# The last batch's tail in a new order on every engine: cross attention with a mixture of experts behind it

## The reference

```python
out = retention(LN(x), ctx, ctx)      # 16 heads of 16, decaying causal scores, chunked in the kernel
x = x + out
x = x + fp8_gemm(LN(x), kernel)       # rounded to e4m3, then a plain product
q, k, v = x_n @ Wq.T, ctx @ Wkv.T     # 16 heads of 16
attn = softmax(q @ k.T * 16 ** -0.5)
x = x + (attn @ v) @ Wproj.T + bproj
logits = LN(x) @ router.T             # 8 experts, the best 4 of each token, softmax over these
gate, up = split(x_n @ gate_up[e].T + b)
act = (clip(up) + 1) * min(gate, 7) * sigmoid(1.702 * gate)
out = x + sum over chosen e of w[e] * (act @ down[e].T + b)
```

## Time and profile before

| | |
|---|---|
| median of three runs | 963.2 us (957.24, 965.97, 963.2) |
| profiled execution, its own time | 960.33 us |
| its span, first to last instruction | 958.5 us |
| mean granted TensorE clock | 0.892 |
| TensorE busy | 785.8 us (82%) |
| VectorE, ScalarE, GpSimd busy | 635.5 (66%), 480.4 (50%), 281.9 us (29%) |

### The profile page before, as it was taken

One profiled execution on the slowest core, in us unless ns is written; L12 is line 12 of the kernel. 1 busy time (PEld: TensorE's weight loads), 2 busy tenths in 40 slices (PEclk: granted clock), 3 DMA queues, 4 the chain that ended last, 5 costly groups with the idle time before them and its releaser, 6 DMA issues. The chain is left out here.

```text
span 958.5 us, 19166 instructions
## 1 busy us (share of the span) xinstructions
PE 785.8 (82%) x6449; PEld 489.9 (51%) x6449; DVE 635.5 (66%) x1288; ACT 480.4 (50%) x977; POOL 281.9 (29%) x260
## 2 busy tenths in 40 slices
PE   0682677779887888998978789779999999999994
PEld 0441333233332533342323225567898889888883
DVE  5545656787658787788688975357667766556552
ACT  1210310445334363435675752545777777777772
POOL 6005100310030100001000004125678566566543
PEclk9996779668989799797998986889999999999997
DMA  8321263013221144010454511032354344343332
GB/s 285 115 72 44 99 198 101 34 43 115 71 68 66 40 121 129 2 51 23 134 167 167 165 39 46 23 134 52 64 134 74 63 69 66 55 70 66 58 42 34
DMA packets 70779, 81.41 MB, mean 85 GB/s; under 512 B 10080, under 2 KB 64224, under 8 KB 70560
## 3 DMA queue, kind: packets, MB, share of 16 engines
q1 hardware_dynamic: 56864, 61.01, 20.1%
q0 software_dynamic: 13824, 19.18, 12.3%
HBM read 51.65 MB, written 28.51 MB: 84 GB/s over the span
## 5 line engine op out<-in xcount | busy, mean ns | idle before, releaser
L381 PE MATMUL gu_ps<-xt_room,w 128*128 128x256 f16 (+1 forms) x2112 | 214.8, 256 | 5.9 <-ACT xt_room L276 5.4
L1170 DVE TENSOR_REDUCE neg_max<-sc 128x2 f32<-128x1024 f32 x128 | 156.4, 1222 | 60.7 <-PE sc L1509 59.8
L381 PEld LDWEIGHTS gu_ps<-xt_room,w 128*128 (+1 forms) x2112 | 178.4, 99 | 31.6 <-issue 8.2
L1802 POOL DMA_INDIRECT out<-y,block_rows x72 | 119.7, 1663 | 78.9 <-ACT y L1771 41.6
L2099 PE MATMUL misc<-w,h_room 128*128 (+1 forms) x864 | 104.0, 278 | 7.5 <-DVE h_room L336 4.9
L2099 PEld LDWEIGHTS misc<-w,h_room 128*128 128x128 f16 x864 | 85.1, 99 | 20.4 <-issue 9.1
L849 POOL COPY rden_rows<-rden 128x512 f32<-128x512 f32 x16 | 10.7, 671 | 276.1 <-DVE rden L1191 243.5
L267 POOL DMA_INDIRECT gx<-xr_d,block_rows x64 | 71.7, 1120 | 39.4 <-DVE share L1975 15.7
L325 DVE TENSOR_SCALAR up<-up 128x512 f32<-128x512 f32 x72 | 32.3, 449 | 69.2 <-ACT up L298 69.0
L956 ACT ACTIVATE h_room<-gu_ps 128x512 f32<-128x512 f32 x88 | 47.8, 596 | 56.6 <-PE gu_ps L1538 56.3
L308 ACT ACTIVATE h_room<-prod_room 128x512 f16<-128x512 f32 x72 | 45.4, 631 | 59.2 <-DVE prod_room L329 59.2
(11 more groups left out here) (294 smaller groups left out, 1288.0 us busy)
## 6 DMA issues: line engine op xcount, KB each, us to landing
raw_next<-in_gate_up_t SPq DMA_DIRECT2D x5, 1024.0 KB, 5.1
stack_d<-t SPq DMA_DIRECT2D x16, 256.0 KB, 2.3
sq<-stack_d SPq DMA_DIRECT2D x16, 192.0 KB, 3.2
kz<-stack_d SPq DMA_DIRECT2D x16, 192.0 KB, 4.2
raw<-in_gate_up_t SPq DMA_DIRECT2D x3, 1024.0 KB, 4.9
raw_next<-in_down_t SPq DMA_DIRECT2D x5, 512.0 KB, 8.3
ctx_pad<-in_ctx SPq DMA_DIRECT2D x4, 512.0 KB, 4.2
ctx_s<-in_ctx_swapped SPq DMA_DIRECT2D x4, 512.0 KB, 5.1
```

Source lines behind the costliest of these rows:

```text
L381: ins = pe.matmul(m.gu_ps[:, 2 * half + g, cols], weights(m, i, r, wi, slice(col, col + P)), m.xt[:, i % 2, kd, xi, own], start=(j == 0 an ...
L1170: dve.tensor_reduce(neg_max[:, qt, :, pair], sc[:], AX.X, ALU.max, negate=True).then_inc(m_max, 1)
L1802: pool.indirect_dma_start(out=out, out_offset=bass.IndirectOffsetOnAxis(ap=block_rows[:, i, r:r + 1], axis=0), in_=y[:, i % 2, r, :], in_o ...
```

## The change

In the first block, for the last batch: list_pre goes one step forward; the one-hots 0 to 3 and list_early go in front of the loop's later steps and of w_low of expert 5, and the one-hots get rooms of their own in the unused tails of the weight tensors, not raw_next. The eight list_rows are spread singly between the scores; o_part 0 and 1 go in front of values 13 and of score 30. early_rows, early_turn and early_gate go behind the loop: TensorE does den 3, den_turn 3, early_turn 0, o_rest 0 and 1, early_turn 1, early_gate (0,0), (0,1), turn4 0, early_gate (1,0), (1,1), turn4 1, (2,0), early_turn 2, route. GpSimd does early_gather 0, den_spread 3, early_gather 1 to 3, root_a 0 and 1. Only glu and up of units 0 and 1 remain in the first block; prod, high and low of all units and the rest of units 2 and 3 move to the second. Turn4_take of the last batch goes from ScalarE to VectorE, the highs of units 0 to 3 from ScalarE to GpSimd, the power on GpSimd becomes an Exp on ScalarE between up 2 and glu 3. Gathers 4 to 7 don't wait for earlier blocks. In the second block TensorE begins with the gates left over, and VectorE has prods and lows between its routing steps.

```diff
     parts["high16"], parts["low16"] = (by_tile(room(E * FIRST // 2).bitcast(F16)) for _ in range(2))
-    parts["low_hot"] = raw_next[:].bitcast(F16).rearrange("p (n l t) -> p n l t", l=P, t=FIRST)
...
+    one_hot = lambda a: a.bitcast(F16).rearrange("p (l t) -> p l t", l=P)
+    n_gx, n_hot = EB * 2 * XW, P * FIRST // 2
+    m.low_first = [one_hot(tails[0][:, n_gx:n_gx + n_hot])] + [one_hot(room(n_hot)) for _ in range(LOW_HOT - 1)]
...
     pool.wait_ge(m.list_ok, i + 1)
-    need(pool, m.x_tr, i - GX + 1)
-    need(pool, m.share_ok, i - GX + 1)
+    if i >= EB + GX:
+        pool.wait_ge(m.x_tr, i - GX + 1)
+        pool.wait_ge(m.share_ok, i - GX + 1)
...
+def take_high_early(pool, m, n):
+
+    pool.wait_ge(m.prod_ok, n + 1)
+    pool.tensor_copy(m.h16[0][:, n % 4].rearrange("p i r -> p (i r)"), m.prod[:, n % 2, :]).then_inc(m.h_hi, 1)
...
+    if n == 4:
+        act.wait_ge(m.h_hi, n)
     act.wait_ge(m.prod_ok, n + 1)
-    if n >= 4:
-        need(act, m.dn_mm, n // 2 - 1)
+    need(act, m.dn_mm, n // 2 - 1)
...
             def turn4_take(b, u):
+                if b == LAST:
+                    return
...
+            def turn4_copy(b, u):
+                if b < LAST:
+                    return
+                dve.wait_ge(tr4, b * 2 + u + 1)
+                need(dve, rt_mm, b)
+                dve.tensor_copy(x4[:, u].rearrange("p k h n -> p (k h n)"), bank("turn4", u).bitcast(F16)).then_inc(t4_ok, 1)
...
                 need(dve, list_mm, e - LOW_HOT + 1)
-                dve.tensor_tensor(lists["low_hot"][:, e % LOW_HOT], lists["low_no"],
+                dve.tensor_tensor(m.low_first[e % LOW_HOT], lists["low_no"],
...
                 pe.wait_ge(list_low, e + 1)
+                if e == EARLY_E:
+                    pe.wait_ge(list_took, 1)
                 for i in range(FIRST):
-                    ins = pe.matmul(sc[:, 1, 256 + e * HI:256 + (e + 1) * HI], lists["low_hot"][:, e % LOW_HOT, :, i],
+                    ins = pe.matmul(sc[:, 1, 256 + e * HI:256 + (e + 1) * HI], m.low_first[e % LOW_HOT][:, :, i],
...
                     pe.wait_ge(list_step, EARLY_STEP)
+                    pe.wait_ge(w_lo, EARLY_E * WP)
...
+            unit(2)
+            act.wait_ge(rt, CHOOSE_STEPS)
+            act.activation(tmp[4][:], tmp[4][:], ACT.Exp).then_inc(rt_exp, 1)
             take_turned(act, m, 2)
-            take_high(act, m, 3)
+            unit(3)
...
-            expo = flat(tmp[4])
-            pool.memset(euler[:], math.e).then_inc(euler_ok, 1)
-            pool.wait_ge(euler_ok, 1)
-            pool.wait_ge(rt, CHOOSE_STEPS)
-            pool.tensor_tensor(expo, euler[:], expo, ALU.pow).then_inc(rt_exp, 1)
+            for n in range(4):
+                take_high_early(pool, m, n)
...
+            put_prod(dve, m, 0)
...
             assert count[0] == CHOOSE_STEPS + 2
+            put_prod(dve, m, 1)
+            put_low(dve, m, 0)
...
             assert count[0] == PLACE_STEPS
-            dve.wait_ge(rt_exp, 1)
-            weigh_experts(dve, done, tmp, chosen[:, :, LAST], combine[:, LAST, :])
-            assert count[0] == PLACE_STEPS + WEIGH_STEPS
+            put_low(dve, m, 1)
...
             low_one_hot(0)
+            put_prod(dve, m, 2)
+            dve.wait_ge(rt_exp, 1)
+            weigh_experts(dve, done, tmp, chosen[:, :, LAST], combine[:, LAST, :])
+            assert count[0] == PLACE_STEPS + 2 + WEIGH_STEPS
...
             list_rows(EB)
-            put_low(dve, m, 3)
-            collect(0)
+            put_low(dve, m, 2)
+            put_prod(dve, m, 3)
...
             take_share(1)
+            collect(0)
+            put_low(dve, m, 3)
...
-            down(0)
+            gate_or_up(pe, m, 2, 1)
+            gate_or_up(pe, m, 3, 0)
...
             ins.then_inc(pre_mm, 1)
+            gate_or_up(pe, m, 3, 1)
             gate_up(2, 0)
+            down(0)
+            list_expert(0)
             turn_x(3)
-            gate_or_up(pe, m, 5, 0)
-            list_expert(0)
-            gate_or_up(pe, m, 5, 1)
+            gate_up(2, 1)
...
 PLACE_STEPS = CHOOSE_STEPS + 7
-LOW_HOT = 4
...
 ORDER = {
-     "o_part": ((), (), (), (1290.5, 1294.5)),
+     "o_part": ((), (), (), (1285.5, 1290.5)),
...
-     "list_pre": ((), (), (), (1245.05,)),
+     "list_pre": ((), (), (), (1243.5,)),
...
-     "list_low": ((), (), (), (1260, 1261, 1262, 1263, 1272, 1275, 1283.1, 1283.2)),
-     "list_rows": ((), (), (), (1264.5, 1265.5, 1268, 1270.5, 1274.5, 1277, 1287, 1287.5)),
-     "list_take": ((), (), (), (1280, 1288)),
-     "list_early": ((), (), (), (1264,)),
+     "list_low": ((), (), (), (1245.6, 1245.7, 1245.8, 1245.9, 1272, 1275, 1283, 1285)),
+     "list_rows": ((), (), (), (1267.5, 1273.5, 1280.5, 1289.5, 1291.5, 1294.5, 1296.5, 1296.7)),
+     "list_take": ((), (), (), (1295.2, 1297)),
+     "list_early": ((), (), (), (1246,)),
...
-     "early_rows": ((), (), (), (1282, 1282.1, 1282.2, 1282.3)),
-     "early_bias": ((), (), (), (1286.2, 1286.3, 1289, 1289.1)),
-     "early_gather": ((), (), (), (1283.1, 1283.2, 1283.3, 1283.4)),
-     "early_turn": ((), (), (), (1294.7, 1304.4, 1311)),
-     "early_take": ((), (), (), (1296.3, 1304.6)),
-     "early_gate": ((), (), (), (1296.5, 1298.5, 1301.5, 1304.2, 1305.2, 1305.9, 1306.7, 1310)),
-     "early_glu": ((), (), (), (1297.5, 1302.5, 1305.72, 1306.7)),
-     "early_up": ((), (), (), (1299.5, 1304.5, 1306.1, 1311)),
-     "early_prod": ((), (), (), (1302.5, 1305.5, 1306.55, 1312)),
-     "early_high": ((), (), (), (1305, 1306.2, 1311.5)),
-     "early_low": ((), (), (), (1304.7, 1306.3, 1313)),
+     "early_rows": ((), (), (), (1295.4, 1295.41, 1295.42, 1295.43)),
+     "early_bias": ((), (), (), (1287.1, 1287.2, 1287.3, 1287.4)),
+     "early_gather": ((), (), (), (1296.1, 1300.5, 1300.6, 1300.7)),
+     "early_turn": ((), (), (), (1301.6, 1304.1, 1311)),
+     "early_take": ((), (), (), (1303.5, 1304.6)),
+     "early_gate": ((), (), (), (1304.2, 1304.3, 1306.65, 1306.7, 1310)),
+     "early_glu": ((), (), (), (1305.75, 1306.75)),
+     "early_up": ((), (), (), (1306.1, 1306.9)),
...
      "o_norm": ((288, 393, 454, 586), (612, 691, 763, 828), (886, 981, 1034, 1080), (1185, 1229, 1281, 1302)),
-     "x_bias": ((134,), (721,), (989,), (1284,)),
+     "x_bias": ((134,), (721,), (989,), (1290,)),
...
      "route_take": ((738,), (1001,), (1199,), (1318,)),
-     "w_low": ((1056, 1063, 1074, 1084, 1085, 1086, 1107, 1113, 1120, 1137, 1145, 1151, 1171, 1190, 1223, 1245.2, 1245.3, 1245.4),),
+     "w_low": ((1056, 1063, 1074, 1084, 1085, 1086, 1107, 1113, 1120, 1137, 1145, 1151, 1171, 1190, 1223, 1272.5, 1276, 1284),),
...
-     "den_turn": ((281, 387, 446, 580), (608, 687, 760, 826), (883, 977, 1027, 1072), (1173, 1221, 1276, 1301)),
+     "den_turn": ((281, 387, 446, 580), (608, 687, 760, 826), (883, 977, 1027, 1072), (1173, 1221, 1279.5, 1301)),
```

More of the change, by code:

```diff
@@ L41 @@
 GX = 4
+LOW_HOT = 4
 WX = ((0, 0), (0, 1), (1, 0))
@@ L139, in route_parts, with list_parts @@
     return parts
-def list_parts(raw, raw_next):
+def list_parts(raw):
     n_no = sum(math.prod(shape) for _, shape in LIST_NO)
@@ L465, in phase_a @@
         route_const = route_parts(consts)
-        lists = list_parts(raw, raw_next)
+        lists = list_parts(raw)
         ctx_n = ctx_pad[:, 0:T * D].rearrange("p (t d) -> p t d", t=T)
@@ L579, in phase_a @@
         ARGS |= {name: range(3) for name in ("early_turn",)}
-        ARGS |= {name: range(EB) for name in ("early_rows", "early_bias", "early_gather", "early_up", "early_glu", "early_high", "early_prod", "early_low")}
+        ARGS |= {name: range(EB) for name in ("early_rows", "early_bias", "early_gather", "early_up", "early_glu")}
         ARGS |= {name: [(n, g) for n in range(4) for g in range(2)] for name in ("early_gate",)}
@@ L982, in _ @@
                  "early_take": lambda b, i: take_turned(act, m, i), "early_glu": lambda b, n: take_gate(act, m, n),
-                 "early_up": lambda b, n: take_up(act, m, n), "early_high": lambda b, n: take_high(act, m, n)})
+                 "early_up": lambda b, n: take_up(act, m, n)})
         @block.vector
@@ L1340, in _ @@
                  "early_bias": lambda b, i: put_bias(dve, m, bias16, m.early_of, m.early_hot[:, 2 * i:2 * i + 2, :], i),
-                 "early_prod": lambda b, n: put_prod(dve, m, n), "early_low": lambda b, n: put_low(dve, m, n),
+                 "turn4_take": turn4_copy,
                  "quantise_weights": quantise_weights, "choose": choose, "weigh": weigh,
@@ L1716, in phase_m @@
         block_rows, share, share_of = m.block_rows, m.share, m.share_of
-        bias_of, euler = sb("bias_of", [P, 2, 8, E]), sb("euler", [P, T * E])
+        bias_of = sb("bias_of", [P, 2, 8, E])
         m.gx = sb("gx", [P, GX, 2, XW])
@@ L1722, in phase_m @@
         bias_in, share_out = sem("bias_in"), sem("m_share_out")
-        euler_ok, rt, rt_exp = sem("euler_ok"), sem("rt"), sem("m_rt_exp")
+        rt, rt_exp = sem("rt"), sem("m_rt_exp")
```

(2 more changed lines are left out.)

## The result

The changed kernel takes 949.99 us (median of 20 runs), the one before 962.84 (20 runs): a ratio of 0.9848, 95% interval 0.9818 to 0.9877, or 14.6 us less by the ratio. The ratio leaves out executions more than 1.5% slower than the fastest of their kernel, 6 of the 20 of the change and 4 of the 20 of before; the two medians of all 20 are 12.9 us apart. The forecast was 951 us, 11 less. Its profiled execution took 951.75 us (span 950.0, granted clock 0.894; before 960.33, 958.5, 0.892).

A forecast was written before the change was run, and what follows sets the result against it. The prediction took the loop's start as decisive, held back by TensorE's idling and half clock between 562 and 655 us. Second block 16.5 us earlier, less 4.3 for its length and 1.0 for copies: 11.2 gained, 951 us, range 944 to 962.

The forecast's parts named there:

- the clock rival: The granted clock falls anyway, with thin work from 571 to 575 us: gain 7, 955 us; chance 25%.
- GpSimd's queue: Gather issues in front of den_spread 3 and root_a cost 4.7 us more: gain 6.5, 954.5 us; chance 12%.
- a slower kernel: TensorE stays at half clock until the loop, 573 to 640 us: net 5 slower, 966 us; chance 7%.
- the case of more: GpSimd's queue is shorter and VectorE's 1.5 us of waits don't come: gain 14 to 16, 946 us; chance 11%.
- One-hots before w_low: First block, last batch: list_rows 0 to 3 don't wait; values 15 ends 9.3 us earlier, about 5 of it clock.
- the root's hold: First block's tail: gathers 1 to 3 hold GpSimd in front of root_a 0, so 2.5 us lost.
- VectorE's turn4 copy: First block's tail: the copy after turn4, moved from ScalarE to VectorE, takes 1.1 us for 1.02.
- taken at once: First block's tail: without early_prod and early_low queued, VectorE starts o_add 0 at 600.1 us for 614.35.
- TensorE's own queue is shorter: 17.7: Second block: TensorE's gates, gate_ups, downs, turn and list take 17.7 us, less than VectorE's queue.
- VectorE's 20.9: Second block: VectorE's work of 17.0 us, 1.5 for waits and 2.43 for seven one-hots make 20.9 us.
- Copies on GpSimd: Second block: four copies cost VectorE 0 to 1.6 us, taken as 1.0; by the lock rule up to 2.4.
- as long as before: The stretch from the loop's first gate_up to the end stays at 308 us.

The follow-up runs named there:

- the run with one number moved: Kernel before, with early_low 0 moved behind stats_a 1 in VectorE's queue so that o_add 0 goes ahead of it: ratio 0.9956.
- with TensorE relieved: Changed kernel, with early blocks 0 to 3 taking expert 0's weights at a constant address, not by register: one execution, 959.38 us.
- the list order: Changed kernel, with list_expert 0 put in front of down 0 in the second block: ratio 0.986.

## Why the prediction was right, step by step

**The size.** 949.99 us for 951 forecast, in the forecast's own range of 947 to 955; neither the clock rival nor GpSimd's queue nor a slower kernel came. The gain was larger than the sum: 12.9 us by the medians, 14.6 by the ratio, which touches the case of more (14 to 16), and 13.6 at the loop for 11.2. Of those 2.4, the end of values 15 gave 1.0 (0.3 of it left at o_add 0), the way from o_add 0 to the second block 1.5, and the second block 0.6, with 21.6 where the sum had 22.2.

**One-hots before w_low, and the clock.** Right: list_rows 0 to 3 don't wait, both o_part take 2.8, the clock is 0.99 to 1.00 until values 15. But the reason was half of it. The prediction named the wait of 1.21 us and the thin work together, and for the rival (the clock falls anyway, 25%) called the thin work the danger. The runs show that this danger is real and that the wait was not what mattered: with the wait gone and list_rows bunched the clock falls (0.50, values +34.8 and +36.4), and with the wait kept and filler among the list_rows it stays. A longer wait can do it too: with w_low first, 2.00 us at den_turn 2. The early one-hots alone, in the order of before, bring 4.2 of the 10.3 us; putting back w_low or the bunched list_rows costs the change 4.0 or 4.5 of them. The rival was kept away by the spreading, which the sum counted only as fewer instructions in front of values 15.

**The o_part inside the loop.** The sum gave the move no price of its own, and it has none.

**The tail.** Right by the reason given: o_add 0 is behind o_rest and nothing else. That its place alone is no gain, the run with one number moved shows; the deferral of prods and lows, which the sum booked as "taken at once", is what the change has besides; no run makes the deferral alone. O_rest took 3.21 for 2.8, at the low clock, as forecast. Too high were the root's hold (2.5; it was 1.4, and moving the gathers gave 1.3) and VectorE's turn4 copy (1.1; it took 0.69).

**The second block.** Here a step failed, though its sum was near: "TensorE's own queue is shorter: 17.7". It was 20.9 us busy, with 0.7 idle. The mis-sized term is the gates: 168 at 1.50 per 24 are 10.5 us, and they took 13.8. The rows held the right price, 48 gates in 4.17 us; the 1.50 came from 24 gates directly behind the eight transposes of turn4, and was taken for the rate. VectorE's 20.9 was too high in turn: it was busy 17.5 where the sum has 19.4 of work, and with TensorE relieved the block takes 19.4. So two errors met, 21.2 forecast and 21.6 measured, with the wrong engine as the bound. That is also why the copies cost nothing and the list order 0.8 instead of the 2.15 that VectorE waits. The Exp was hidden, as said.

**Copies on GpSimd.** 1.0 taken; VectorE lost 0.6, the block at most 0.2. The Trainium skill ("SBUF — State Buffer", section "SBUF: two separate sides") would have the later one stand still for the whole of the other, 0.61 a copy, up to 2.4 in all, for a gain of 9.8. The measured 0.6 lies within that bound: two of the four copies held VectorE up, and these two were longer themselves (0.74 and 1.01 us for 0.61), so both sides lost.

**The loop** took 308.7 and 311.9 us for 308.1. Over all runs it is 307.5 to 310.9 (mean 308.7, four traces) in the kernels with the second block of before, and 307.8 to 311.9 (mean 309.7, ten traces) in those with the second block of the change. So "as long as before" is not refuted, but a loop longer by about 1 us isn't excluded either. The spread is as large as most single edits: position at the start of the loop tells them apart, the total doesn't.

## What to carry to other kernels

Where the granted clock is low in a busy stretch, look at what TensorE did before it fell, not only at its waits; the cure that cost nothing here was to put the thin products one at a time between dense ones. Take the price of a product from the longest run of its kind in the trace, and ask whether its address is a constant or looked up. When work is moved out of a tail, sum each engine's queue where it lands, and move all of it: a single operation that jumps the queue meets the next one.

## What was not expected of the hardware

Products of 128 columns whose weights are addressed by a register took 88 ns each in a run (72 in 6.33 us), and 62.5 ns where 24 stood directly behind eight transposes (24 in 1.50, at 613.46); with a constant address they took 59 in the long run too (48 in 2.84 us). With 256 columns the looked-up address costs next to nothing: the 24 products of a down take 2.82 us with it and 2.78 with a constant. Why those 24 are fast was not tried. Not every pause does it: the gates behind 0.82 us in which TensorE waited for its sequencer take 91 ns each. The granted clock fell to 0.50 behind 14.5 us in which TensorE was busy 13.63, so a busy engine is no proof against it. And it differs from execution to execution at one and the same place: from +5 to +10 it is 0.58 and 0.61 in two traces whose code is the change's up to there, and 1.00 in the others, for 1.6 to 1.8 us at the end of values 15.
